# Rope rotation read from PSUM on VectorE, beside the cosine product on GpSimd, in an attention and LoRA kernel

## The reference

```python
x = layernorm(x0)
q, k, v = heads(x @ w_q), heads(x @ w_k), heads(x @ w_v)        # 32, 8 and 8 heads of 128
lk, lv  = heads((x @ w_lq) @ w_lk), heads(x @ w_lv)             # 32 heads of 128
rope(t) = t * cos + rotate_half(t) * sin                        # for q, k and lk
rotate_half(t) = concat([-t[..., 64:], t[..., :64]])
attn = causal_softmax(q @ k.T / sqrt(128)) @ v                  # k, v repeated 4 times
lat  = causal_softmax(q @ lk.T / sqrt(128)) @ lv
x1 = x0 + attn @ w_o + lat @ w_lo
out = x1 + ffn(layernorm(x1))      # base linear layer + 8 routed LoRA adapters of rank 16
```

## Time and profile before

| | |
|---|---|
| median of 3 runs | 2166.24 us (2165.63 to 2167.49) |
| profiled execution, its own time | 2170.34 us |
| its span on the core | 2168.5 us |
| TensorE busy | 2085.7 us, 96%, 11236 matmuls |
| VectorE busy | 1582.2 us, 73% |
| ScalarE busy | 1140.5 us, 53% |
| GpSimd busy | 883.6 us, 41% |
| DMA | 84.34 MB, mean 39 GB/s |

### The profile page before, as it was taken

The page is one execution under the profiler, slowest core; times in us unless marked ns, Lnnn a source line. Parts: engine busy times, 40 slices in busy tenths (PEclk is TensorE's granted clock), DMA queues, the critical chain, the costliest instruction groups (busy, mean ns, idle before and its releaser), DMA issues.

```text
span 2168.5 us, 37857 instructions
## 1 busy us (share of the span) xinstructions
PE 2085.7 (96%) x11236; PEld 1761.5 (81%) x11236; DVE 1582.2 (73%) x2946; ACT 1140.5 (53%) x2502; POOL 883.6 (41%) x693
## 2 busy tenths in 40 slices
PE   5999999999999999999999999999999999999989
PEld 4888878888788887888788887888878888888877
DVE  6677767777777777777777776777777777777775
ACT  2555545555455554555455554555545555555541
POOL 4334443334534344433533444333453334444311
PEclk9999999999999999999999999999999999999999
DMA  2111111111111111112111111111111111111121
GB/s 95 31 35 41 36 32 41 39 39 44 29 41 27 41 46 31 37 36 41 36 36 34 39 37 32 41 41 37 45 27 41 27 41 46 30 41 31 41 50 39
DMA packets 101898, 84.34 MB, mean 39 GB/s; under 512 B 28200, under 2 KB 73896, under 8 KB 101680
## 3 DMA queue, kind: packets, MB, share of 16 engines
q1 hardware_dynamic: 101680, 81.65, 15.9%
HBM read 79.26 MB, written 2.36 MB: 38 GB/s over the span
## 4 chain that ended last, share of the span: by engine, by line
PE 72%; DVE 14%; issue 8%; POOL 3%; ACT 2%; DVEq 0%; DMA 0%; ACTq 0%; SPq 0%; POOLq 0%
PE scores L415 9%; PE scores L417 8%; PE scores L416 8%; PE bankT L477 8%; PE bankX L415 7%; PE bankX L417 7%; PE bankX L416 7%; PE bankO L415 5%; PE bankO L417 5%; PE bankO L416 5%; DVE rot_half L980 3%; DVE rot_half L979 3%; DVE probs L963 3%; DVE PT_lo L969 2%; POOL KT_lo L1191 1%
## 5 line engine op out<-in xcount | busy, mean ns | idle before, releaser
L703 ACT ACTIVATE PT_hi<-bankT 128x512 fp32r<-128x512 f32 (+2 forms) x640 | 336.2, 532 | 413.7 <-PE bankO L417 353.2
L969 DVE TENSOR_TENSOR PT_lo<-bankT,PT_hi 128x512 fp32r<-128x512 f32 (+2 forms) x640 | 387.4, 609 | 184.5 <-ACT PT_hi L703 179.4
L762 ACT ACTIVATE probs<-probs,nmax 128x128 f32<-128x128 f32 (+7 forms) x512 | 394.8, 773 | 140.1 <-DVE nmax L963 139.7
L963 DVE CUSTOM_DVE_ANT_0 probs<-scores,mask 128x128 f32<-128x128 f32 (+7 forms) x512 | 381.1, 750 | 62.2 <-PE scores L417 59.9
L477 PE MATMUL bankT<-ident,probs 128*128 128x128 f32 x2304 | 379.2, 273 | 5.7 <-DVE PT_lo L969 2.2
L477 PEld LDWEIGHTS bankT<-ident,probs 128*128 128x128 f32 x2304 | 285.3, 140 | 73.1 <-DVE PT_lo L969 18.1
L1197 POOL TENSOR_TENSOR rot<-rot,cos 128x512 f32<-128x512 f32 x144 | 185.3, 1287 | 227.8 <-DVE rot_half L980 227.8
L1191 POOL TENSOR_TENSOR OT_lo<-o_raw,OT_hi 128x512 fp32r<-128x512 f32 x64 | 82.7, 1291 | 403.3 <-ACT OT_hi L703 403.3
L1199 POOL TENSOR_TENSOR rot<-rot,rot_half 128x512 f32<-128x512 f32 x144 | 207.3, 1439 | 11.3
L703 ACT ACTIVATE OT_hi<-o_raw 128x512 fp32r<-128x512 f32 x128 | 80.9, 632 | 187.0 <-DVE o_raw L1034 180.5
L979 DVE TENSOR_TENSOR rot_half<-rot,sin 64x512 f32<-64x512 f32 x144 | 108.7, 755 | 82.9 <-ACT rot L703 79.5
(11 more groups left out here) (241 smaller groups left out, 5213.2 us busy)
## 6 DMA issues: line engine op xcount, KB each, us to landing
inv_b<-inverses SPq DMA_DIRECT2D x128, 256.0 KB, 4.1
stage<-in_L_attn_w_q SPq DMA_DIRECT2D x32, 256.0 KB, 4.7
stage<-in_L_attn_w_lv SPq DMA_DIRECT2D x32, 256.0 KB, 2.8
stage<-in_L_attn_w_o SPq DMA_DIRECT2D x32, 256.0 KB, 4.6
stage<-in_L_attn_w_lo SPq DMA_DIRECT2D x32, 256.0 KB, 2.6
acc<-in_L_attn_hidden_states SPq DMA_DIRECT2D x2, 1024.0 KB, 6.6
stage<-in_L_attn_w_k SPq DMA_DIRECT2D x8, 256.0 KB, 4.8
stage<-in_L_attn_w_v SPq DMA_DIRECT2D x8, 256.0 KB, 4.9
```

Source lines behind the costliest of these rows:

```text
L703: return act.activation(place, src, ACT.Copy)
L762: act.activation(prob_tile(c, t), prob_tile(c, t), ACT.Exp, bias=nmax[:, c, t:t + 1], scale=-1.0, accum_out=rsum[:, c, t:t + 1]).then_inc( ...
L963: dve.tensor_tensor_reduce(place, src, tile_view(mask[:, S - width:S], c), -SCALE, -MASKED, ALU.add, ALU.min, nmax[:, c, t:t + 1]).then_in ...
L969: dve.tensor_tensor(pt_place(1, hh, w, j), bankT[j % 2][:, block_columns(c, j):CH], f32(pt_place(0, hh, w, j)), ALU.subtract).then_inc(pt_ ...
```

## The change

- VectorE's `rotate` reads the product in its PSUM bank, not `rot`. It still waits for `rope_raw`, ScalarE's copy.
- The bank is free for TensorE when `rope_raw` and `rope_half` have both counted, in the loop and before it.
- The rotations of LK and K stand in their own slot, after the slot's block, and no longer in the next slot.
- GpSimd's cosine product waits for `rope_raw` and not for `rope_half`; the sum behind it waits for `rope_half`.

```diff
@@ bank_x_taken
             if name in ROPE:
                 eng.wait_ge(rope_raw, rope_no(g, h2, name, n) + 1)
+                eng.wait_ge(rope_half, rope_no(g, h2, name, n) + 1)
@@ TensorE, before the loop
-                        pe.wait_ge(*((rope_raw, x + 1) if x < 2 else (x_free, x - 1)))
+                        if x < 2:
+                            pe.wait_ge(rope_raw, x + 1)
+                            pe.wait_ge(rope_half, x + 1)
+                        else:
+                            pe.wait_ge(x_free, x - 1)
...
             pe.wait_ge(rope_raw, 4)
+            pe.wait_ge(rope_half, 4)
@@ VectorE
-            def rotate(no, slot, n, place=None):
+            def rotate(no, n, bank, place=None):
...
                 dve.wait_ge(rope_raw, no + 1)
                 t = slice(n * CH, (n + 1) * CH)
-                dve.tensor_tensor(rot_half[0:HALF, half, :], rot[HALF:HD, slot, :], sin[HALF:HD, t], ALU.mult)
-                dve.tensor_tensor(rot_half[HALF:HD, half, :], rot[0:HALF, slot, :], sin[0:HALF, t], ALU.mult)\
+                dve.tensor_tensor(rot_half[0:HALF, half, :], bank[HALF:HD, :], sin[HALF:HD, t], ALU.mult)
+                dve.tensor_tensor(rot_half[HALF:HD, half, :], bank[0:HALF, :], sin[0:HALF, t], ALU.mult)\
                     .then_inc(rope_half, 1)
@@ VectorE, piece
-                    rotate(rope_no(g, hh, name, n), rope_no(0, hh, name, n) % RING, n)
+                    rotate(rope_no(g, hh, name, n), n, banksX[bank])
@@ VectorE, end of a slot
-                        if here.get(s - 1, ("", 0))[0] in ("LK", "K"):
-                            piece(g, hh, w, s - 1, *here[s - 1], piece_bank(hh, w, s - 1, more))
+                        if s in here and here[s][0] in ("LK", "K"):
+                            piece(g, hh, w, s, *here[s], piece_bank(hh, w, s, more))
@@ VectorE, before the loop (and likewise rotate 1 to 3)
-            rotate(0, 0, 0, 0)
+            rotate(0, 0, four[0], 0)
@@ GpSimd, rope_add
-                pool.wait_ge(rope_half, no + 1)
+                pool.wait_ge(rope_raw, no + 1)
                 pool.tensor_tensor(rot[:, slot, :], rot[:, slot, :], cos[:, chunk(n)], ALU.mult).then_inc(rope_cos, 1)
                 pool.wait_ge(rope_cos, no + 1)
+                pool.wait_ge(rope_half, no + 1)
                 pool.tensor_tensor(rot[:, slot, :], rot[:, slot, :], rot_half[:, half, :], ALU.add).then_inc(rope_sum, 1)
```

More of the change, by code:

```diff
@@ L1109, in _ @@
             normalised_lo(0, 7)
-            rotate(1, 1, 0, 1)
+            rotate(1, 0, four[1], 1)
             latent_lo(0)
@@ L1113, in _ @@
             value_copy(4, 0, 1)
-            rotate(2, 2, 1, 0)
-            rotate(3, 0, 1, 1)
+            rotate(2, 1, four[0], 0)
+            rotate(3, 1, four[1], 1)
             latent_lo(1)
```

## The result

| | before | after |
|---|---|---|
| median | 2166.86 us | 2230.19 us (2229.83 to 2231.93, 4 runs) |
| ratio | | 1.029, interval 1.0273 to 1.0308 |
| span of the profiled execution | 2168.5 us | 2228.0 us |
| VectorE busy | 1582.2 us | 1488.9 us |
| TensorE busy | 96% | 94% |

The change makes the kernel 63 us slower. The forecast was 2227 us, +61.

The account below looks back on a forecast made before the run. TensorE, busy 96% of the span, was taken as the bound. Terms 34.7 - 2.4 + 16.8 + 6.5 + 5.7 = 61 us on 2166.2 gave 2227 us; their range was 38 to 78 us, likeliest 2203 to 2248 us.

Parts of the forecast that it names:

- Part 1: VectorE's rotation from PSUM: always 1.39 us, also beside GpSimd; VectorE loses 70 us of busy time, little reaching the end.
- Rival (c): Rotation from PSUM stretched beside the cosine product as from SBUF: 1 us more at 70 places, 2297 us; chance 0.03.
- Part 2, Q: Q0 to Q1: TensorE 1.12 us late 31 times, 34.7 us; wait for `o_raw` goes at pass ends, -2.4 us.
- Part 2, K: K1 to V0: TensorE starts V0 2.4 us late, 7 times, 16.8 us.
- Part 2, LK: Latent-key windows: LV0 late, less the vanished wait for V^T; 26 x 0.25 = 6.5 us and 6 x 0.95 = 5.7 us.
- Part 3: Row maxima: last exponential delayed 0.5 us by the moved rotations, but hidden behind LV0 with 0.25 us to spare.
- Rival (b): Cover for the late exponential is gone and TensorE waits for it: 2243 us, or 2262 at a full rotation; chance 0.08.
- Part 4: GpSimd's order: cosine product no longer waits for the rotation, a rope ready at most 1.3 us earlier; counted as nothing.
- (a): Slower, but TensorE doesn't meet the moved LK rotations, so those windows only win 0.64 us: 2195 us; chance 0.08.
- (e): TensorE is held by something else anyway, so the later bank release changes nothing: 2166 us; chance 0.02.
- the term of -2.4: Last head of a pass: TensorE's 0.34 us wait for `o_raw` goes, 7 times, -2.4 us.
- Rival (d): Rotation ends before TensorE returns to the bank; only waits for V^T and `o_raw` go: 2143 us; chance 0.03.

Follow-up runs that it names:

- from_sbuf: cos_late with the rotation reading ScalarE's copy in SBUF again, the bank still held through the rotation: 2268.03 us, 1.0469 of the kernel before.
- q1_bank: The changed kernel with window 3's pieces taking the two banks in the other order, so Q1 doesn't wait for Q0's rotation: 2194.2 us, 1.0124.
- k_early: The changed kernel with the rotations of K0 and K1 ahead of their slot's block on VectorE, not behind it: 2215.21 us, 1.0219.
- move_only: from_sbuf with the bank free after ScalarE's copy in the loop; only the move of LK and K rotations is left: 2174.94 us, 1.0033.
- cos_late: The changed kernel with GpSimd's cosine product waiting for the rotation (rope_half) again: 2232.57 us, 1.0294 of the kernel before.
- early_q1: The changed kernel with the edits of early and q1_bank together: 2163.55 us, 0.9983 of the kernel before.
- early: k_early with LK's rotations also ahead of their slot's block: 2200.8 us, 1.0156 of the kernel before.
- lk0_only: The kernel before with LK0's rotation alone moved to its own slot: 2144.95 us, 0.9893; once more 2143.57 us, 0.9884.

## Why the prediction was right

- **Part 1** (1.39 us for a rotation, never stretched): shown, by the rotation's rows after and by from_sbuf. Rival (c) is out. The rule of the Trainium skill ("SBUF — State Buffer", "Who interferes with whom") held here: with one SBUF input the rotation was never slowed beside GpSimd (694 ns at most in 288).
- **Part 2, Q** (34.7 less 2.4 = 32.3): 32.2 measured, of which 31 x 1.17 = 36.3 is Q1 and about -4 the seven pass ends. The wait for `o_raw` goes there as forecast. The wait for `QT_lo` was to stay as it was, and rises from 3.8 to 6.9 us, yet a pass end gains 0.5 us and not 0.34. The two small misses cancel. q1_bank gives 36 us back. The step was to read the distance from the copy's end to the next product, 0.35 us, against the 1.4 us of the rotation, and to see that the chain behind it moves along.
- **Part 2, K** (7 x 2.4 = 16.8): the wait was right to 0.05 us, the term too small by 7 us. What failed is that I priced only the wait and took TensorE's clock as given. An idle stretch as long as this one is longer than any the loop of the kernel before had, so its rows could not show it. Measured: 1.3 to 1.6 us each in five of seven passes; k_early takes the wait down and no low stretch is left in the loop.
- **Part 2, LK** (26 x 0.25 and 6 x 0.95): some 0.14 and 0.9 measured. LV0 was late as forecast (0.92 us for 0.93). I took the wait of 0.64 us for V^T as the gain, with 0.05 us for a restart of TensorE, a figure that no row shows; 0.88 us went, so the restart is 0.24. The term is 4 us too large, the K term 7 too small, and that the sum came out nearly right is in part luck.
- **Part 3** (hidden, 0.25 us to spare): in the changed kernel the exponential of the window above started at 520.88 and ended 0.6 us ahead of LV0's end, and TensorE does not wait for it. It is hidden only because LV0 itself is late. move_only takes that cover away, and there exponentials hold TensorE 35 times, 16.2 us in all. Rival (b) is out for this kernel: its transposes wait for exponentials 3 times, 1.8 us, as before.
- **Part 4** (GpSimd's order is free): shown by cos_late.
- Rivals (a) and (e) are out by the waits above: TensorE does meet the rotations of LK and all the others.
- The range: 38 to 78 us leaves out the term of -2.4; with it the same bounds give some 35 to 75. The measured 63 lies in both.
- Rival (d), faster, needed a gap of 1.45 us behind the copy. early_q1 shows what it takes: with the gaps made, the same idea ends 4 us under the kernel before.

What stays open: why two of seven passes keep the clock after the same idle time. The rows do not tell.

## What to carry to other kernels

Before an engine reads a PSUM bank itself instead of another's copy, look at what TensorE does with that bank next: the reader's time is added to the hold, and if the next product stands closer than that, each instance costs the difference on the bounding engine. Work taken from an engine that is not the bound (93 us of VectorE here) buys nothing. And an order in a queue can be worth more than the work in it: one rotation a slot earlier, with nothing else changed, gave 1.1%.

## What the runs showed of the hardware that I had not expected

- After about 2.5 us of idling in an otherwise dense run, TensorE came back at 1.2 GHz for more than 3 us in five of seven cases of the changed kernel, six of seven in cos_late and four of seven in q1_bank. After 3.4 us (from_sbuf) it did in six of seven, in four of them for twice as long. After 1.66 us (k_early, early, early_q1) it did in none of 21. Between these it goes either way: at the loop's back-edge lk0_only waited 1.8 to 1.9 us in two passes (827.4 and 1591.6) and 1.3 to 1.5 in the other four, and only behind those two is the clock low; the changed kernel idled as long there in two passes (325.2, 591.8) and kept its clock. TensorE in lk0_only, behind two back-edges of the long kind and one of the short:

```profile
828.80:832.00 3.20, 3.20 (x11) 0.53 0.04 6
1593.40:1596.60 3.20, 3.20 (x11) 0.53 0.13 10
573.00:576.00 3.00, 3.00 (x19) 1.00 0.06 11
```

- The lower clock at the start of the kernel comes and goes between executions. It may be part of why single executions of the kernel before ran from 2164 to 2171 us; no run here separates that.
- Two VectorE instructions of 64 partitions that read a PSUM bank take 693 and 683 ns, as from SBUF without a neighbour (689).
- GpSimd can be the one that is slowed. Of its 144 sums (line 1199 before) 54 took over 1.33 us in the kernel before, up to 1.79, each beside a rotation from SBUF. With the rotation from PSUM none did.
